# A decoder layer's cross-attention on one NeuronCore: the inverse of the softmax sums taken once per distinct value, six query slots, and one weighing group a step

## The reference, cut to what matters

```python
def _L0_xattn_ref(q, k, v):          # q = layernorm(x), k = v = ctx_2048
    b, d, m = q.shape
    h = 8
    qh = q.reshape(b * h, d // h, m); kh = k.reshape(b * h, d // h, -1); vh = v.reshape(b * h, c // h, -1)
    qk = jnp.einsum('bdm,bdn->bmn', qh, kh) * scale
    sm = jax.nn.softmax(qk, axis=-1)
    return jnp.einsum('bmn,bcn->bcm', sm, vh).reshape(b, c, m)
```

## Time and profile before

| what | value |
|---|---|
| median of 3 runs | 940.01 us |
| the profiled execution | 940.92 us, its span 939.1 us |
| busy PE, DVE, ACT, POOL over the span | 817.6, 719.0, 458.8, 388.2 us |
| mean granted TensorE clock | 0.953 |
| stage d, from its first ACT copy to the first load of stage e | 522.3 to 748.5 us |

### The profile page before, as it was taken

How to read it: one execution, slowest core, us unless ns; L and a number is a source line. 1 busy time by engine, 2 the same in 40 slices (tenths; PEclk the granted TensorE clock), 3 DMA queues, 4 the chain that set the end, 5 groups by cost and what they waited for, 6 DMA issues and landing times. The chain is left out here.

```text
span 939.1 us, 15123 instructions
## 1 busy us (share of the span) xinstructions
PE 817.6 (87%) x4738; PEld 417.5 (44%) x4786; DVE 719.0 (77%) x2014; ACT 458.8 (49%) x791; POOL 388.2 (41%) x304
## 2 busy tenths in 40 slices
PE   2999488989999999996886589999998568999997
PEld 2888234444444444443765344433443123444443
DVE  7544499878888888880677689989998368999894
ACT  2566046655666666664222444545454135445542
POOL 1456398979200000000122366667666423334331
PEclk9999679999999999998999699999999879999999
DMA  7886645454232322212699355555554214644643
GB/s 271 322 283 247 193 134 151 147 156 145 55 82 56 79 60 75 62 40 77 229 314 322 124 162 159 173 161 154 161 156 112 76 37 100 122 110 102 123 108 89
DMA packets 137103, 134.51 MB, mean 143 GB/s; under 512 B 87232, under 2 KB 99136, under 8 KB 133952
## 3 DMA queue, kind: packets, MB, share of 16 engines
q1 hardware_dynamic: 111488, 104.18, 37.9%
q10 hardware_dynamic: 23808, 16.78, 6.4%
q0 software_dynamic: 1728, 12.58, 4.0%
HBM read 89.65 MB, written 33.03 MB: 131 GB/s over the span
## 5 line engine op out<-in xcount | busy, mean ns | idle before, releaser
L578 DVE CUSTOM_DVE_ANT_0 b_junk<-b_p,mask_qk 128x128 bf16<-128x128 f32 (+3 forms) x512 | 233.2, 489 | 48.2 <-PE b_p L634 46.6
L538 ACT ACTIVATE b_probs<-b_p 128x512 f32<-128x512 f32 (+1 forms) x352 | 184.6, 558 | 113.7 <-PE b_p L658 112.5
L634 PE MATMUL b_p<-b_ks,b_qs 96*128 96x128 bf16 (+3 forms) x512 | 158.9, 317 | 22.3 <-DMA b_ks<-k_parts 11.3
L656 PE MATMUL b_p<-b_qs,b_ks 98*128 98x512 bf16 (+1 forms) x352 | 129.1, 369 | 2.5 <-DMA b_qs<-b_mrow 1.4
L1005 ACT ACTIVATE d_probs<-d_p 128x512 f32<-128x512 f32 x128 | 74.4, 595 | 106.6 <-PE d_p L1111 106.6
L764 POOL TENSOR_SCALAR c_veps<-c_mv 128x1 f32<-128x1 f32 x16 | 6.9, 432 | 256.7 <-DVE c_mv L813 256.7
L634 PEld LDWEIGHTS b_p<-b_ks,b_qs 96*128 96x128 bf16 x512 | 50.3, 99 | 124.0 <-DVE b_mx L578 77.6
L673 PE MATMUL b_pv<-b_probs,b_vs 128*32 128x192 f32 (+3 forms) x1280 | 102.8, 397 | 0.0
L978 POOL TENSOR_TENSOR d_halves<-d_probs 128x1024 f32<-128x1024 f32 x32 | 76.3, 2384 | 54.2 <-ACT d_probs L1005 54.0
L1029 DVE TENSOR_REDUCE d_mx<-d_p 128x1 f32<-128x512 f32 x128 | 83.7, 670 | 19.2 <-PE d_p L1094 17.5
L1375 PE MATMUL e_pg<-wg,e_xt 128*128 128x512 bf16 x250 | 66.1, 384 | 19.1 <-DMA e_xt<-e_xq 18.8
(11 more groups left out here) (142 smaller groups left out, 1532.2 us busy)
## 6 DMA issues: line engine op xcount, KB each, us to landing
k<-in_ctx SPq DMA_DIRECT2D x64, 128.0 KB, 2.7
qh<-x_normed_high SPq DMA_DIRECT2D x64, 128.0 KB, 2.8
q_parts<-a_parts SPq DMA_DIRECT2D x16, 384.0 KB, 3.3
b_qs<-q_parts SPq DMA_DIRECT2D x32, 192.0 KB, 3.4
a_x<-in_x SPq DMA_DIRECT2D x4, 1024.0 KB, 5.5
a_wst<-in_w_gate SPq DMA_DIRECT2D x4, 1024.0 KB, 6.5
a_wst<-in_w_up SPq DMA_DIRECT2D x4, 1024.0 KB, 8.0
a_wst<-in_w_down SPq DMA_DIRECT2D x4, 1024.0 KB, 8.6
```

Source lines behind the costliest of these rows:

```text
L538: nc.scalar.activation(pblock(s2 % 2, kb)[:, j0:j0 + nj, :], p2[(len(EXPS) * s2 + n) % BANKS][:, 0:nj * w].rearrange("p (j c) -> p j c", j ...
L578: nc.vector.tensor_tensor_reduce(out=junk[:, block % UNROLL, 0:w], in0=p1_bank(u, k)[:, 0:w], in1=keep["mask_qk"][:, SEQ - w:], scale=1.0, ...
L634: nc.tensor.matmul(p1_bank(u, k)[:, 0:w], qs[0:STACK, u, j, qt * P:(qt + 1) * P], ks[0:STACK, u, 0:w], start=True, stop=True).then_inc(p1_ ...
L656: nc.tensor.matmul(bank, ks[0:STACK + 2, s2, kb * P:(kb + 1) * P], qs[0:STACK + 2, s2, j0:j0 + nj, kb * P:], start=True, stop=False)
```

## The change

Stage d is written as one loop over `i` with the head or pair of each piece of work given by its lag (`pair_ready(i, n)` is pair p where i = 2p + n).

- The query rows have six slots instead of four. Six heads are loaded at the end of stage c, and after that head i+1 in step i.
- The order on SP is another: the row of maxima first, then context, then queries, then what belongs to pairs.
- The sums: ACT copies `pd` to SBUF (`den`), two DMAs on ACT's queue spread one row of each head over 8 partitions of 64 values (`few`, 16 x 64 for the pair), DVE inverts those in one instruction, SP stores them to DRAM (`inv`, a step or two later), and two further DMAs on SP read them back into all 64 rows of each head (`rden`).
- The weighted sums: ACT copies `pn` to SBUF (`raw`), and DVE multiplies `raw` by `rden`, both in SBUF, in step 2p + 9.
- PE weighs after the four score blocks of a step and no longer between them: two groups in each step, the sums of a pair behind them in odd steps. The probabilities have five slots instead of four.
- Some buffers of earlier stages are placed and released otherwise to make room.

```diff
+def load_query_rows(sp, scr, keep, head):
+
+    slot, landed = head % QSLOTS, keep["q_in"][head % UNROLL]
...
 def output_projection(nc, io, scr, keep):
...
-            for s in range(UNROLL * XROWS // P):
+            for s in range(QSLOTS * XROWS // P):
                 sp.wait_ge(stored[s], 48)
-            for i in range(UNROLL):
-                load_query_rows(sp, scr, keep, i, i)
+            for i in range(QSLOTS):
+                if i >= UNROLL:
+                    sp.wait_ge(keep["q_in"][i % UNROLL], 48)
+                load_query_rows(sp, scr, keep, i)
...
 def cross_attention(nc, io, scr, keep):
...
-        probs = m.sb("probs", [P, UNROLL, KD, DIM]); halves = m.sb("halves", [P, 2, DIM]); total = m.sb("total", [P, UNROLL, DIM])
+        probs = m.sb("probs", [P, PSLOTS, KD, DIM]); halves = m.sb("halves", [P, 2, DIM]); total = m.sb("total", [P, UNROLL, DIM])
-        rden = m.sb("rden", [P, 2, DIM]); y = m.sb("y", [P, 2, DIM]); x1 = m.sb("x1", [P, 2, DIM]); x2 = m.sb("x2", [P, 2, DIM])
+        den = m.sb("den", [P, 2, DIM]); few = m.sb("few", [2 * RUNS, 2, H]); inv = m.sb("inv", [2 * RUNS, 2, H])
+        raw = m.sb("raw", [P, 2, DIM]); rden = m.sb("rden", [P, 2, DIM]); y = m.sb("y", [P, 2, DIM]); x1 = m.sb("x1", [P, 2, DIM]); x2 = m.sb("x2", [P, 2, DIM])
...
         @block.sync
         def _(sp):
+            for i in range(LAST):
+                j = i - 3
+                if 0 <= j < STEPS:
+                    sp.wait_ge(p1_used, use(j + 2, TURN) + 1)
+                    if j == 0:
                         sp.wait_ge(padded, 2)
+                    sp.dma_start(ql[H:H + 1, j % QSLOTS, :].bitcast(F32), mrow[:, j % UNROLL, :].bitcast(F32)).then_inc(m_in[j % UNROLL], 16)
+                if 2 <= i < STEPS:
+                    sp.wait_ge(kl_done, i - 1)
+                    sp.wait_ge(kh_done, i - 1)
+                    load_context_rows(sp, io, keep, i % 2, i)
+                j = i + 1
+                if QSLOTS <= j < STEPS:
+                    sp.wait_ge(scores, KD * (j - QSLOTS + 1))
+                    sp.wait_ge(q_in[j % UNROLL], 48 * (j // UNROLL))
+                    load_query_rows(sp, scr, keep, j)
+                p = pair_ready(i, 8)
+                if p is not None:
+                    sp.wait_ge(inv_done, p + 1)
+                    sp.dma_start(scr["inv"][2 * RUNS * p:2 * RUNS * (p + 1), :], inv[:, p % 2, :]).then_inc(inv_out, 16)
+                p = pair_ready(i, 5)
+                if p is not None:
+                    if due(p - 1):
+                        sp.wait_ge(weighted, p - 1)
                     for a in range(2):
+                        sp.dma_start(vt[:, 2 * (p % 2) + a, :, :], io["ctx_t"][bass.ds(2 * p + a, 1)].rearrange("o (k p) c -> p (o k) c", p=P)
+                                     ).then_inc(vt_in[p % 2], 16)
+                p = pair_ready(i, 7)
+                if p is not None:
+                    if due(p - 1):
+                        sp.wait_ge(x2_done, p - 1)
+                    sp.dma_start(x1[:, p % 2, :], scr["x1"][bass.ds(P * p, P), :]).then_inc(x1_in[p % 2], 16)
+                p = pair_ready(i, 12)
+                if p is not None:
+                    sp.wait_ge(x2_done, p + 1)
+                    sp.dma_start(scr["x2"][bass.ds(P * p, P), :], x2[:, p % 2, :]).then_inc(x2_out[p % 2], 16)
+                p = pair_ready(i, 9)
+                if p is not None:
+                    sp.wait_ge(inv_out, 16 * (p + 1))
+                    if due(p - 1):
+                        sp.wait_ge(y_done, p - 1)
+                    for a in range(2):
+                        at = RUNS * (2 * p + a)
+                        sp.dma_start(rden[a * H:(a + 1) * H, p % 2, :], scr["inv"][at:at + RUNS, :].rearrange("r c -> (r c)")
+                                     .unsqueeze(0).broadcast_to([H, DIM])).then_inc(rden_in, 16)
...
         @block.scalar
         def _(act):
+            for i in range(LAST):
+                j = i - 3
 
                 def exponential(n):
+                    if not 0 <= j < STEPS:
                         return
+                    if n == 0 and j >= PSLOTS:
+                        act.wait_ge(weighted, (j - PSLOTS) // 2 + 1)
+                    act.wait_ge(scores, KD * j + n + 1)
+                    nc.scalar.activation(probs[:, j % PSLOTS, n, :], p2[(KD * j + n) % BANKS][:], ACT.Exp, scale=SCALE).then_inc(exps, 1)
 
                 exponential(0)
+                p = pair_ready(i, 6)
+                if p is not None:
+                    act.wait_ge(summed, p + 1)
+                    if due(p - 1):
+                        act.wait_ge(few_in, 32 * (p - 1))
+                    nc.scalar.activation(den[:, p % 2, :], pd[:], ACT.Copy).then_inc(den_kept, 1)
+                if i < STEPS:
+                    act.wait_ge(k_in[i % 2], 32 * (i // 2 + 1))
                     if due(KD * (i - 3)):
                         act.wait_ge(scores, KD * (i - 3))
+                    nc.scalar.activation(kk[:, i % UNROLL, :], k2[:, i % 2, :], ACT.Copy).then_inc(kk_done, 1)
                 exponential(1)
+                if p is not None:
+                    act.wait_ge(den_kept, p + 1)
+                    if due(p - 1):
+                        act.wait_ge(inv_done, p - 1)
+                    if due(p):
+                        act.wait_ge(few_in, 32 * p)
+                    for a in range(2):
+                        act.dma_start(few[a * RUNS:(a + 1) * RUNS, p % 2, :],
+                                      den[a * H:a * H + 1, p % 2, :].rearrange("o (r c) -> o r c", r=RUNS)).then_inc(few_in, 16)
                 exponential(2)
+                p = pair_ready(i, 8)
+                if p is not None:
+                    act.wait_ge(weighted, p + 1)
+                    if due(p - 1):
+                        act.wait_ge(y_done, p - 1)
+                    nc.scalar.activation(raw[:, p % 2, :], pn[:], ACT.Copy).then_inc(raw_kept, 1)
+                if i < STEPS:
+                    nc.scalar.activation(kh[0:H, i % UNROLL, :], k2[0:H, i % 2, :], ACT.Copy).then_inc(kh_done, 1)
                 exponential(3)
...
         @block.vector
         def _(dve):
...
-                def invert(pr, s, part):
-                    if live(pr, PAIRS):
-                        at = slice(part * P, (part + 1) * P)
-                        dve.wait_ge(summed, pr + 1)
-                        if part == 0 and due(pr - 1):
-                            dve.wait_ge(y_done, pr - 1)
-                        nc.vector.reciprocal(rden[:, s, at], pd[:, at]).then_inc(rden_done, 1)
...
+                maximum(1)
+                if i < STEPS:
+                    dve.wait_ge(kk_done, i + 1)
+                    nc.vector.tensor_tensor(kk[H:P, i % UNROLL, :], k2[H:P, i % 2, :], kk[H:P, i % UNROLL, :].bitcast(F32),
+                                            ALU.subtract).then_inc(kl_done, 1)
+                p = pair_ready(i, 9)
+                if p is not None:
+                    dve.wait_ge(rden_in, 32 * (p + 1))
+                    dve.wait_ge(raw_kept, p + 1)
+                    if due(p - 1):
+                        dve.wait_ge(x2_done, p - 1)
+                    nc.vector.tensor_tensor(y[:, p % 2, :], raw[:, p % 2, :], rden[:, p % 2, :], ALU.mult).then_inc(y_done, 1)
+                maximum(2)
+                maximum(3)
+                p = pair_ready(i, 6)
+                if p is not None:
+                    dve.wait_ge(few_in, 32 * (p + 1))
+                    if due(p - 1):
+                        dve.wait_ge(inv_out, 16 * (p - 1))
+                    nc.vector.reciprocal(inv[:, p % 2, :], few[:, p % 2, :]).then_inc(inv_done, 1)
...
         @block.tensor
         def _(pe):
...
+                def weigh(p, nb):
                     if nb == 0:
+                        if due(p):
+                            pe.wait_ge(raw_kept, p)
+                        pe.wait_ge(vt_in[p % 2], 32 * (p // 2 + 1))
+                    for a in range(2):
+                        j = 2 * p + a
+                        if nb == 0:
+                            pe.wait_ge(exps, KD * (j + 1))
+                        last = nc.tensor.matmul(pn[a * H:(a + 1) * H, :], vt[:, j % UNROLL, nb, :], probs[:, j % PSLOTS, nb, :],
                                                 start=nb == 0, stop=nb == KD - 1, skip_group_check=True)
                     if nb == KD - 1:
                         last.then_inc(weighted, 1)
+
+                def sum_probs(p):
+                    pe.wait_ge(totalled, 2 * (p + 1))
+                    if due(p):
+                        pe.wait_ge(den_kept, p)
+                    for a in range(2):
+                        last = nc.tensor.matmul(pd[a * H:(a + 1) * H, :], keep["ones64"][:], total[:, (2 * p + a) % UNROLL, :], start=True, stop=True)
+                    last.then_inc(summed, 1)
+
                 for n in range(KD):
                     first_scores(n)
                     second_scores(n)
```

(67 more changed lines are left out.)

217 lines of the change are left out of this document (63 added, 154 removed).

## The result

The changed kernel takes 935.93 us in the median (20 runs, 932.48 to 945.31), against 940.48 for the kernel before on the same chips (20 runs, 938.55 to 950.48 and one stray of 1187.26): a ratio of 0.9952, interval 0.9929 to 0.9974. It is faster by 4.5 us, half a percent, where 14.2 were forecast. The profiled execution took 934.68 us with a span of 932.9; the one of before had 940.92 and 939.1. The traces thus differ by 6.2 us; the other 1.7 is scatter (the profiled execution of after lies 1.25 under its median, that of before 0.44 over the median of its 20).

A forecast was written before the change was run, and what follows sets the result against it. PE and DVE were taken to share the bound. Beginning -3.0, regular stretch -13.1, drain -2.3 and end +4.2 sum to -14.2 us: 925.8 against 940.0, likeliest 926, range 914 to 940.

The forecast's parts named there:

- The raw wait: Even steps: PE's weighing waits 1.4 us for ACT's copy of raw out of the only bank `pn`.
- signs of being wrong: DVE's product waiting each pair for a DMA, PE waiting before its transposes, or pairs taking over 13 us.
- Regular stretch: First to fifteenth pair's sums: 11.0 + 13 x 12.2 = 169.6 us against 182.75, so -13.1 us.
- SP's circle: SP's issues, rden load, product, last maxima, transpose, SP's next odd step: 11.8 us a pair, below 12.2, costing nothing.
- ACT's chain: Even step: raw copied behind exponential 2 delays PE's weighing; step 6.4 us, pair 12.2 us, the new bound.
- Beginning: Start of stage d: six slots end step 5's query wait, first sums then wait for POOL; -3.0 us.
- Drain: After the fifteenth pair's sums: sums, exponential 3 and POOL take 8.9 us instead of 11.21; -2.3 us.
- End: Last sums to stage e's first load: the DRAM round trip makes 8.75 us into 13.0; +4.2 us.
- the early raw copy: Rival, 18%: raw comes early and loads land in 2.7 us; pair 11.4 us, kernel 916.
- Dear issues: Rival, 15%: issues cost more on ACT beside a full DMA load; pair 12.9 us, kernel 935.
- Late rden: Rival, 17%: rden loads land at 5.5 us, stalling DVE in odd steps; pair 14.0 us, kernel 949.
- The product against POOL: Rival, 8%: DVE's product, both operands in SBUF, waits for one POOL `total` each pair; kernel 939, no change.

The follow-up runs named there:

- raw early: Changed kernel with ACT's copy of the weighted sums moved ahead of exponential 0 in even steps; 12.12 us a pair, 933.05 us, ratio 0.9895.
- rden early: Changed kernel with SP's two rden loads moved to right behind the context rows; 12.31 us a pair, 936.67 us, ratio 0.9948.
- grouping alone: Kernel before with only PE's order changed: in even steps four score blocks, then four weighing groups; 11.55 us a pair, 916.32 us, ratio 0.9727.
- three moves: Changed kernel with raw copied first, rden loaded earlier, and vt and x1 loads issued by ACT, not SP; 11.43 us a pair, 928.14 us, ratio 0.9837.
- filling in stage d: Changed kernel with query rows of heads 4 and 5 loaded in stage d's first two steps, not in stage c; 936.67 us, ratio 0.9959.
- raw and rden early: Changed kernel with both the raw copy moved first and the rden loads moved behind the context rows; 11.86 us a pair, 930.42 us, ratio 0.9877.
- six slots: Kernel before with only the query slots raised to six, filled as in the change; 13.11 us a pair, 943.22 us, ratio 1.0017.

## Why the prediction was wrong

The direction was right; the size was a third. The traces show -6.2 of the forecast -14.2. The missing 8.0 us are 3.0 in the regular stretch, 2.8 in the beginning, 1.1 in the drain and 1.0 behind the stage. The raw wait came as forecast, but one of the prediction's own signs of being wrong came too: DVE's product waits for a DMA in 12 of 16 pairs (1.48 us at 669.82, 19.2 in all), where "a few tenths" were allowed.

**Regular stretch**: forecast -13.1, measured -10.06. The step that failed is SP's: "Just below ACT's 12.2, so it costs nothing", with "SP's own load is 19 issues of 0.5 to 0.6, some 10.8 us a pair: below too". The queue is full for 11.95 us, at 0.63 an issue with its gap, not 0.56. The second rden load is issued 6.5 us after the maxima row, not 5.8, and SP's circle alone measured 12.12 (raw early), where the forecast was 11.8. ACT's chain alone measured 12.31 (rden early) for 12.2; raw started at 4.00, not 3.85. The two together made 12.38. Of the 13 x 0.18 = 2.3 us some 1.4 are thus ACT's chain and 0.9 SP's circle beside it. The first pair has no raw to wait for, as forecast, but took 11.74 for 11.0, 0.7 more; what holds it wasn't isolated. PE's step ("10.8 us a pair if PE waits for nothing") was exact: 151.55/14 = 10.8.

**What bounds the kernel before** was read wrongly, though it changed no term: DVE's parts were added up to "12.6 us of 13.05". A sum of means counts overlap twice: three maxima of 0.68 us in a row take 1.88 us (657.92 in the kernel after). The window has 162.4/14 = 11.6 us busy, and cutting 3.2 of it gave 0.38. The gain is PE's order. What came with it costs 0.83 us a pair against grouping alone (12.38 against 11.55), and more at the end. The three moves (raw first, rden early, three issues off SP) take 0.95 back, so most of that cost lies in the new path's copies, loads and issues and where they stand; no run took the inverses' path out alone. This is why the change brings so little.

**Beginning**: forecast -3.0, measured -0.16. This is the term with the largest error for its size. The query rows' wait went as said, but "the sums wait for POOL (last exponential of head 1 at about 539, plus 3.8 us)" took POOL for idle. POOL's timeline in the kernel after:
```profile
537.28 2.39 POOL L970 TENSOR_TENSOR d_halves<-d_probs 128x1024 f32<-128x1024 f32 x1 [7.81 <-ACT d_probs L994]
539.75 1.61 POOL L974 TENSOR_TENSOR d_total<-d_halves 128x512 f32<-128x512 f32 x1
541.51 2.40 POOL L970 TENSOR_TENSOR d_halves<-d_probs 128x1024 f32<-128x1024 f32 x1
543.99 1.60 POOL L974 TENSOR_TENSOR d_total<-d_halves 128x512 f32<-128x512 f32 x1
```
It works for 8.3 us in a row on two heads from 537.28, so the sums can't be before 545.6. In before POOL's second total ended at 543.06 + 1.28 = 544.34, 1.46 us ahead of the sums: no more than that was to be had for the wait of 2.74 us, and 1.13 came. The wait had cost PE more than its length, which the prediction did not see either: behind it the products of step 5 ran at half the clock (the entry of 0.50 in this window of before; after has 1.00 in 541 to 545).
```profile
542.00:545.00 3.00, 3.00 (x9) 2.32 (x8) 2.60 (x5) 1.71 (x3) 2.26 (x2) 0.50 0.79 255
```
"The six additional loads in stage c lie under its last stores: nothing" is open: stage d starts 0.97 us later in after, and starts in the traces lie up to 17 us apart (518.2 to 535.5) for reasons ahead of the stage; the 0.61 that filling in stage d gave back is within that scatter.

**Drain**: forecast -2.3, measured -1.24. The path was right, exponential 3 and then POOL, but both were too short. Exponential 3 ended 5.8 us after the sums (724.13), not 5.1, because exponential 2 was held for 0.87 us by the issues on ACT and raw stood between the two; POOL's additions took 4.0 and not 3.8. The weighing's wait for raw (2.20 us at 723.70) is beside this path: PE was through 0.94 us before POOL.

**End**: forecast +4.2, measured +4.19. The chain is the forecast one, but its terms agree only in their sum, which is luck: the store took 1.35 us and not 2.3, the issues and landing of `few` 3.15 and not 2.75, rden 3.63 and not 3.26. The chain of raw beside it, 0.7 us shorter, was not in the forecast. Behind the stage there is 1.0 us more, for which there was no term and no cause was found.

Of the rivals, the early raw copy (916) did not come. The run with that copy ahead, in which rden's loads still land after some 3.1 us, has 12.1 and not 11.4 us a pair: SP stood behind it. Dear issues came in their price (0.63 us each on ACT's queue, not 0.45) and not in their effect: exponential 2 at 661.89 waited 0.36 us for PE and not for them, and the pair is 12.38, not 12.9. Late rden happened in its place but not its size: loads land after 3.1 us in the median (2.7 to 3.6), not 5.5. The product against POOL happened rarely (mean 797 ns, once 2.47 us beside halves at 724.65). With rden early alone it did not happen (691 ns), but with raw and rden early the mean is 1228 ns over twelve pairs: when its data come decides whether it meets POOL. The rule of the Trainium skill ("SBUF — State Buffer", on the shared port pair) named in the prediction agrees with these durations, as in the earlier trace rows.

## What to carry to other kernels

Take an engine's load from the busy time of a window, never from counts times mean durations; and ask of a busy engine what its neighbours wait for before crediting its relief. When a change combines a reordering with a new path through DRAM, price each alone: here the reordering alone was worth some 25 us, and with the path beside it 4.5 were left. Count the issues on a DMA queue like work on an engine, and treat a chain that is estimated 3% below the bound as being the bound.

## What was unexpected of the hardware

One weighing group between two blocks of scores costs PE far more than in a row: 16 matmuls in one go took 3.65 us (four groups, 0.91 each, or 0.86 from one to the next), where a group alone between blocks cost 1.22 us; PE's busy time a pair fell by 1.1 us with the same matmuls. Why is not shown. DVE's subtraction and maxima got shorter (1141 to 855 ns, 670 to 658) from PE's order alone, with no change to DVE. Issues that follow each other on SP's queue cost 0.63 us each, 11.95 us for 19; two on ACT's queue took 0.63 each beside the exponentials, where I had 0.45. After waits of PE between 1.2 and 3.4 us the granted clock of what followed was 0.50 to 0.68 in several places (before at 542 and at the last sums, six slots at 545, after at 732), and the same 16 matmuls took 5.35 us in place of 3.65. After others it stayed at 1.00: the 2.20 us at 723.70 in after, and 2.71 us at 744.05 with rden early. So the length of the wait alone does not decide it.
